# Where the empty rows are written: one scatter per group of the ranking, or all of them in the first softmax

## What is computed

```python
K, Q, V = typed_linear(x, Wk, ...), typed_linear(x, Wq, ...), typed_linear(x, Wv, ...)
att,   v   = edge_msgs(K[row], Q[col], V[row], e1, e2)   # row = src, col = dst
att_i, v_i = edge_msgs(K[col], Q[row], V[col], e2, e1)   # the inverse edges
att   = seg_softmax(att, col, n)      # over the edges with the same dst
att_i = seg_softmax(att_i, row, n)    # over the edges with the same src
agg = segment_sum(v * att, by=col) + segment_sum(v_i * att_i, by=row)
...
return _layernorm(x + layer(agg, x))
```

## Time and profile before

| | us |
|---|---|
| median of 3 runs | 9991.26 |
| lowest, highest | 9989.2, 9998.15 |
| profiled execution | 9994.34 |
| its span, first to last instruction | 9992.6 |

### The profile page before, as it was taken

The page is one execution under the profiler, slowest core; times in us unless marked ns, Lnnn a source line. Parts: engine busy times, 40 slices in busy tenths (PEclk is TensorE's granted clock), DMA queues, the critical chain, the costliest instruction groups (busy, mean ns, idle before and its releaser), DMA issues. The chain is left out here.

```text
span 9992.6 us, 137436 instructions
## 1 busy us (share of the span) xinstructions
PE 6360.8 (64%) x34016; PEld 4321.0 (43%) x34017; DVE 6541.9 (65%) x13906; ACT 4360.4 (44%) x13243; POOL 5689.7 (57%) x5436
## 2 busy tenths in 40 slices
PE   3778666666665577677767677621677643899543
PEld 1257444444443344444444444410555432677322
DVE  1068999999997566666666666652555537888523
ACT  0100433344433455555555555521555543888411
POOL 4230777777777577777777777756888800000022
PEclk6655555555555788888888888865988877999755
DMA  3110000000000788888888888876999994787510
GB/s 100 43 51 2 8 9 9 9 9 9 9 9 9 244 262 261 263 259 261 260 261 258 261 260 258 255 197 210 334 332 332 322 131 135 254 259 258 197 43 23
DMA packets 1355142, 1664.99 MB, mean 167 GB/s; under 512 B 418366, under 2 KB 1154898, under 8 KB 1354722
## 3 DMA queue, kind: packets, MB, share of 16 engines
q1 hardware_dynamic: 854746, 958.02, 29.4%
q0 software_dynamic: 260288, 671.32, 21.8%
q10 hardware_dynamic: 239946, 34.12, 3.3%
HBM read 1059.06 MB, written 641.81 MB: 170 GB/s over the span
## 5 line engine op out<-in xcount | busy, mean ns | idle before, releaser
L1118 PE MATMUL exch_pG<-exch_tab,exch_ohT 128*128 x3328 | 1528.4, 616 | 953.7 <-ACT exch_kc L1040 949.3
L1541 PE MATMUL sum_pS<-sum_row,sum_oh 128*128 128x260 f32 x6656 | 1670.8, 408 | 698.3 <-issue 292.3
L985 POOL DMA_INDIRECT exch_row<-table,exch_of x1664 | 1676.2, 1007 | 551.0 <-issue 507.9
L830 POOL DMA_INDIRECT recs<-place_rec,place_addr x1568 | 1598.5, 1019 | 509.2 <-issue 485.6
L1541 PEld LDWEIGHTS sum_pS<-sum_row,sum_oh 128*128 128x128 f32 x6656 | 1309.7, 202 | 1059.0 <-issue 856.0
L1118 PEld LDWEIGHTS exch_pG<-exch_tab,exch_ohT 128*128 128x128 f32 x3328 | 768.1, 242 | 1696.8 <-issue 1502.2
L1580 DVE TENSOR_TENSOR sum_row<-sum_row,agg_al 128x1792 f32<-128x1792 f32 x416 | 841.4, 2023 | 510.1 <-DMA sum_row<-spill 496.9
L1199 POOL DMA_INDIRECT bys<-sum_pb x768 | 949.5, 1236 | 273.6 <-issue 225.3
L1199 POOL DMA_INDIRECT bys<-exch_pb x832 | 841.2, 1011 | 312.2 <-issue 248.2
L1563 ACT ACTIVATE sum_off<-kept_ramp,sum_neg 128x128 f32<-128x128 f32 x3328 | 1017.6, 388 | 0.0
L784 DVE SCALAR_TENSOR_TENSOR place_junk<-place_pB,place_own_g,sort_tri 128x128 bf16<-128x128 f32 x3136 | 879.8, 347 | 15.3 <-issue 15.2
(11 more groups left out here) (297 smaller groups left out, 12097.1 us busy)
## 6 DMA issues: line engine op xcount, KB each, us to landing
spill<-exch_row SPq DMA_DIRECT2D x208, 1024.0 KB, 5.1
sum_row<-spill SPq DMA_DIRECT2D x208, 1024.0 KB, 7.8
sum_row<-bys SPq DMA_DIRECT2D x208, 1024.0 KB, 4.9
mid<-exch_pb SPq DMA_DIRECT2D x208, 528.0 KB
sum_pb<-mid SPq DMA_DIRECT2D x192, 528.0 KB, 4.6
exch_row<-table,exch_of POOLq DMA_INDIRECT x1664
recs<-place_rec,place_addr POOLq DMA_INDIRECT x1568
bys<-exch_pb POOLq DMA_INDIRECT x832
```

Source lines behind the costliest of these rows:

```text
L830: nc.gpsimd.indirect_dma_start(recs, bass.IndirectOffsetOnAxis(addr[:, par, 0, t:t + 1], 0), rec[:, par, t, :], None, bounds_check=last_sl ...
L985: nc.gpsimd.indirect_dma_start(row[q][:, t, TD:TD + S.TW], None, table, bass.IndirectOffsetOnAxis(of[q][:, t:t + 1], 0), bounds_check=last ...
L1118: nc.tensor.matmul(pG[t % 3][:, 0:VK], ohT[ring(j, 2)][:, t, :], flat[:, bass.ds(tiles[t] * GW, VK)], start=True, stop=True).then_inc(s_ga ...
L1541: last = nc.tensor.matmul(pS[h * HG + t // 2][:, 0:AW], oh[h][:, t, :], row[j][:, t, :], start=(t % 2 == 0), stop=(t % 2 == 1))
```

## The change

The counting stage works out the same list of empty slots, now in a tile `pad_at`, and SyncE writes it to a new DRAM tensor, `free`. The placing stage no longer scatters empty rows: no four ahead of group 0, no 17th scatter in a group, no copy of 128 slot numbers on ScalarE, no tile `none`, and the waits count 16 scatters. In the first softmax SyncE loads the list ahead of the keys, VectorE fills a tile `none` with the empty row ahead of its other work, and GpSimd scatters it 102 times, ahead of the 64 scatters that it has there. At the end of that stage GpSimd waits for these too.

```diff
@@ -493,7 +493,9 @@
                 sp.dma_start(r[:, n * w:(n + 1) * w, :], padrec[:]).then_inc(s_pad, 16)
             sp.wait_ge(s_hc, 3)
             sp.dma_start(otile1, otile[1][:]).then_inc(s_pad, 16)
-            sp.wait_ge(s_pad, 144)
+            sp.wait_ge(s_free, 1)
+            sp.dma_start(free, pad_at[:]).then_inc(s_pad, 16)
+            sp.wait_ge(s_pad, 160)
 
         @block.scalar
         def _(act):
...
@@ -580,7 +582,7 @@
                     link(nc.vector.tensor_scalar(pad_h[:], pad_h[:], 7, None, ALU.logical_shift_right))
                     link(nc.vector.scalar_tensor_tensor(out=pad_l[:], in0=pad_l[:], scalar=float(NT), in1=pad_h[:],
                                                         op0=ALU.mult, op1=ALU.add))
-                    link(nc.vector.tensor_tensor(k.padslot[:], pad_l[:], pad_off[:], ALU.add))
+                    nc.vector.tensor_tensor(pad_at[:], pad_l[:], pad_off[:], ALU.add).then_inc(s_free, 1)
 
                 dve.wait_ge(s_ot, d + 1)
                 for n in range(4):
...
@@ -646,9 +647,6 @@
             s.sem(n) for n in ("stage", "oh", "rowp", "rows", "tps", "tlo", "l", "selr", "addr", "link", "turn", "rec", "whole")]
         s_b, s_eq, s_cnt, s_cur, s_low = [[s.sem(f"{n}{d}") for d in range(2)] for n in ("b", "eq", "cnt", "cur", "low")]
         s_scat = [s.sem(f"scat{p}") for p in range(2)]
-        none = s.sb("none", [P, S.RC])
-        pad_at = s.sb("pad_at", [P, 2, 1], I32)
-        s_none, s_pads = s.sem("none"), s.sem("pads")
         block = ctx.enter_context(nc.Block())
 
         @block.scalar
...
@@ -677,8 +675,7 @@
                 if more:
                     act.wait_ge(s_addr, g + 1)
                     stage(g + 1, 1 - par)
-                act.wait_ge(s_scat[par], i * (16 * (SG + 1)))
-                nc.scalar.activation(pad_at[:, par, :], k.padslot[:, bass.ds(g, 1)], ACT.Copy)
+                act.wait_ge(s_scat[par], i * (16 * SG))
                 nc.scalar.activation(rec[:, par, :, 0:3], ln[:, bass.ds(g * SG, SG), :], ACT.Copy)
                 nc.scalar.activation(rec[:, par, :, S.OWN], own[:, 0, bass.ds(g * SG, SG)], ACT.Copy)
                 nc.scalar.activation(rec[:, par, :, S.LO], piece[:, 0, 0, bass.ds(g * SG, SG)], ACT.Copy)
...
@@ -751,9 +748,6 @@
 
         @block.vector
         def _(dve):
-            nc.vector.memset(none[:], 0.0).then_inc(s_none, 1)
-            dve.wait_ge(s_none, 1)
-            nc.vector.memset(none[:, S.SC + S.H:S.SC + S.H + 1], -1.0).then_inc(s_none, 1)
             nc.vector.memset(rec[:], 1.0)
             nc.vector.memset(piece_g[:], 0.0).then_inc(s_addr, 1)
             nc.vector.memset(slot[:], 0.0).then_inc(s_selr, 1)
...
@@ -803,7 +797,7 @@
                 nc.vector.tensor_scalar(slot_l[:], slot_i[:], P - 1, None, ALU.bitwise_and)
                 link(nc.vector.tensor_scalar(slot_i[:], slot_i[:], 7, None, ALU.logical_shift_right))
                 link(nc.vector.scalar_tensor_tensor(out=slot[:], in0=slot_l[:], scalar=float(NT), in1=slot_i[:], op0=ALU.mult, op1=ALU.add))
-                dve.wait_ge(s_scat[par], i * (16 * (SG + 1)))
+                dve.wait_ge(s_scat[par], i * (16 * SG))
                 link(nc.vector.tensor_tensor(addr[:, par], slot[:], bc(inval[:, bass.ds(g * SG, SG)], 1, 2), ALU.add))
                 nc.vector.tensor_copy(rec[:, par, :, S.SLOT].bitcast(I32), addr[:, par, 1, :]).then_inc(s_addr, 1)
                 assert n_link[0] == PER, n_link
...
@@ -812,15 +806,6 @@
         @block.gpsimd
         def _(pool):
             last_slot = nc.gpsimd.to_reg(P * NT - 1)
-
-            def pad(at, sem):
-                nc.gpsimd.indirect_dma_start(bys, bass.IndirectOffsetOnAxis(at, 0), none[:], None,
-                                             bounds_check=last_slot, oob_is_err=False).then_inc(sem, 16)
-
-            pool.wait_ge(s_none, 2)
-            pool.sem_inc(s_turn, 1)
-            for n in range(NG, S.NPC):
-                pad(k.padslot[:, n:n + 1], s_pads)
 
             def body(g, par, i, more):
                 pool.wait_ge(s_rec, g + 1)
@@ -830,11 +815,9 @@
                     nc.gpsimd.indirect_dma_start(recs, bass.IndirectOffsetOnAxis(addr[:, par, 0, t:t + 1], 0),
                                                  rec[:, par, t, :], None, bounds_check=last_slot,
                                                  oob_is_err=False).then_inc(s_scat[par], 16)
-                pad(pad_at[:, par, :], s_scat[par])
             in_turns(pool, NG, body)
-            pool.wait_ge(s_pads, 16 * (S.NPC - NG))
             for par in range(2):
-                pool.wait_ge(s_scat[par], (NG // 2) * 16 * (SG + 1))
+                pool.wait_ge(s_scat[par], (NG // 2) * 16 * SG)
 
 
 def angle_table(nc, k, S, s, w_time, b_time, blk):
...
@@ -1225,7 +1208,9 @@
         s_in, s_a, s_dve, s_sub, s_exp, s_c, s_t, s_e, s_f, s_k, s_x = [
             s.sem(n) for n in ("in", "a", "dve", "sub", "exp", "c", "t", "e", "f", "k", "x")]
         if bys is not None:
-            s_turn = s.sem("turn")
+            s_turn, s_none, s_free, s_pads = [s.sem(n) for n in ("turn", "none", "free", "pads")]
+            none = s.sb("none", [P, S.RC])
+            pad_at = s.sb("pad_at", [P, S.NPC], I32)
             pb = [s.sb(f"pb{n}", [P, S.LATER, S.RC]) for n in range(8)]
             s_pb, s_sc = [[s.sem(f"{n}{j}") for j in range(8)] for n in ("pb", "sc")]
         block = ctx.enter_context(nc.Block())
@@ -1235,6 +1220,8 @@
         @block.sync
         def _(sp):
             kv = keys.rearrange("t e -> (t e)")
+            if bys is not None:
+                sp.dma_start(pad_at[:], free).then_inc(s_free, 16)
             sp.wait_ge(s_k, 1)
             sp.dma_start(key[:, 1:C + 1], kv[0:SPn * C].rearrange("(p c) -> p c", p=SPn)).then_inc(s_in, 16)
             if SPn > 1:
...
@@ -1272,6 +1259,12 @@
         def _(pool):
             if bys is not None:
                 last_slot = nc.gpsimd.to_reg(P * S.NT - 1)
+                pool.wait_ge(s_none, 2)
+                pool.wait_ge(s_free, 16)
+                pool.sem_inc(s_turn, 1)
+                for n in range(S.NPC):
+                    nc.gpsimd.indirect_dma_start(bys, bass.IndirectOffsetOnAxis(pad_at[:, n:n + 1], 0), none[:], None,
+                                                 bounds_check=last_slot, oob_is_err=False).then_inc(s_pads, 16)
                 for n in range(S.AHEAD):
                     pool.wait_ge(s_pb[n % 8], 16 * (n // 8 + 1))
                     pool.sem_inc(s_turn, 1)
@@ -1279,6 +1272,7 @@
                         forward(nc, S, pb[n % 8], t, bys, last_slot).then_inc(s_sc[n % 8], 16)
                 for n in range(8):
                     pool.wait_ge(s_sc[n], 16 * S.LATER * (S.AHEAD // 8))
+                pool.wait_ge(s_pads, 16 * S.NPC)
 
         @block.scalar
         def _(act):
...
@@ -1294,6 +1288,10 @@
         @block.vector
         def _(dve):
             link, _ = chain(dve, s_dve)
+            if bys is not None:
+                nc.vector.memset(none[:], 0.0).then_inc(s_none, 1)
+                dve.wait_ge(s_none, 1)
+                nc.vector.memset(none[:, S.SC + S.H:S.SC + S.H + 1], -1.0).then_inc(s_none, 1)
             link(nc.vector.memset(zero[:], 0.0))
             link(nc.vector.memset(key[:, 0:1], -2.0))
             nc.vector.memset(key[:, C + 1:C + 2], -2.0).then_inc(s_k, 1)
...
@@ -1836,6 +1834,7 @@
     mid = nc.dram_tensor("mid", [P, S.NT, S.RC], F32, kind="Internal").ap()
     bys = nc.dram_tensor("bys", [P * S.NT, S.RC], F32, kind="Internal").ap()
     runs = nc.dram_tensor("runs", [P, S.NT, S.H + 1], F32, kind="Internal").ap()
+    free = nc.dram_tensor("free", [P, S.NPC], I32, kind="Internal").ap()
     otile1 = nc.dram_tensor("otile1", [1, S.NT], I32, kind="Internal").ap()
     keys = [nc.dram_tensor(f"keys{d}", [S.NT2, P], F32, kind="Internal").ap() for d in range(2)]
     att = [nc.dram_tensor(f"att{d}", [S.NT2, S.H, P], F32, kind="Internal").ap() for d in range(2)]
```

More of the change, by code:

```diff
@@ L419, in one_hots, with sort_edges @@
     return last
-def sort_edges(nc, k, S, src, dst, edge_attr, recs, otile1, bys):
+def sort_edges(nc, k, S, src, dst, edge_attr, recs, otile1, free):
     CT, SG, NO = S.CT, S.SG, S.NO
@@ L471, in count_owners @@
         pad_h = s.sb("pad_h", [P, NPC], I32)
+        pad_at = s.sb("pad_at", [P, NPC], I32)
         pH = [s.pb(f"pH{d}") for d in range(2)]
         pO = [s.pb(f"pO{n}") for n in range(4)]
-        s_in, s_ea, s_dve, s_c, s_oh, s_h, s_hc, s_o, s_oc, s_ot, s_rec, s_pad, s_prep = [
-            s.sem(n) for n in ("in", "ea", "dve", "c", "oh", "h", "hc", "o", "oc", "ot", "rec", "pad", "prep")]
+        s_in, s_ea, s_dve, s_c, s_oh, s_h, s_hc, s_o, s_oc, s_ot, s_rec, s_pad, s_prep, s_free = [
+            s.sem(n) for n in ("in", "ea", "dve", "c", "oh", "h", "hc", "o", "oc", "ot", "rec", "pad", "prep", "free")]
         block = ctx.enter_context(nc.Block())
@@ L612, in _, with place_edges @@
                 last.then_inc(s_ot, 1)
```

(9 more changed lines are left out.)

7 lines of the change are left out of this document (3 added, 4 removed).

## The result

The changed kernel takes 10043.1 us (median of 6 runs, 10035.8 to 10048.5), the kernel before 9990.2 beside it (6 runs): ratio 1.0054, 95% interval 1.0041 to 1.0067. It is slower by some 53 us; 37 were forecast. The profiled run takes 10048.3 us, with a span of 10046.6 where the earlier trace rows has 9992.6. In a later batch it was 1.0060 (1.0041 to 1.0079).

A forecast was written before the change was run, and what follows sets the result against it. Placing was taken as bound by a two-group loop through the scatters' landing, near GpSimd's own rate. Terms −89.7 − 1.3 − 0.4 + 0.7 + 128.0 gave +37.3 us, 10028.6 us on the median; range 9983 to 10060.

The forecast's parts named there:

- part 4: First softmax: 102 uncovered scatters at 1.276 us add 130.2, an earlier start takes off 2.2; sum +128.0 us.
- part 5: First softmax: exponentials wait behind loads needing scatter 134, but weights are out near 6890, hidden before GpSimd ends at 6911.
- part 1: Placing: without 98 pad scatters the two-group loop falls from 22.555 to 21.63 us a group, gaining 89.7 us, plus 1.3.
- The landing of a record scatter: Placing: time from a record scatter's end until ScalarE may start; 1.28 us forecast, bounds 1.13 and 1.58.
- The hold: Placing: GpSimd scatters held while VectorE builds one-hots; 1.08 us a group forecast, bounds 0.33 and 1.36.
- The rule of the Trainium skill: Placing: VectorE wouldn't stop descriptor writing, so hold 0, step 21.09 us and whole change about −15 us.
- Placing, mean step: Placing: group-to-group step falls from 22.555 to 21.63 us over 97 steps, gaining 89.7 us.
- Start: Before the first record scatter: dropped `none` fills −0.4 us, the list's store in counting +0.7.
- A: Rival: placing gains nearly all, holds 0.33, quick landing, step 21.2 us; whole −4 us, 9987; chance 27 in 100.
- B: Rival: VectorE's own 20.88 us sets placing's step; stage gains 162, whole −35 us, 9956; chance 7 in 100.
- C: Rival: landing 1.58, hold 1.36, placing step 21.92 us; whole +65, 10057; chance 64 in 100 together with the forecast.
- D: Rival: the removed scatter wasn't on placing's path, which gains nothing; whole +128, 10119; chance 2 in 100.

The follow-up runs named there:

- the rows in both places: Kernel before with its placing scatters kept, plus all 102 empty-row scatters in the first softmax: 10123.3 us, ratio 1.0125.
- four buffers: Changed kernel with four buffers of `rec` and `addr` in placing instead of two, loop body of four groups: 10051.1 us, ratio 1.0048 to the kernel before.
- the spread one: Changed kernel with 41 of 102 empty-row scatters moved from the first softmax to two other stages; other chips: 12167.9 and 12172.3 us, ratios 0.9937 and 0.9943.
- 17 scatters: Changed kernel plus a seventeenth 32-byte-row scatter per group in placing, to an unread spare tensor; another chip: 12365.7 us, kernel before 12258.5.

## Why the prediction was right, and where it was off

Sign and range held; the size was 37 for 53. That it comes so near is in part luck: by the profiles the terms of the change and its surroundings add up to 63 us, and an output stage that no term spoke of takes 11 off again.

- **Softmax, part 4**: +128.0 forecast, +128.9 by the profiles, +128.3 with the rows in both places. That the 102 scatters have no cover and that VectorE's scans take in as many scatters as before (102 of them take 1417 ns on average, the 64 behind them 976) was read rightly: the time over 0.973 us a scatter is 45.3 us in all, before (64 scatters) as after (102). The first scatter comes 2.84 us after the stage's first DMA, for 4.02 before; that is −1.2 where −2.2 was forecast. The exponentials come 222 us after the stage's start (215 forecast), behind ScalarE's last loads, and GpSimd is still the last: part 5 holds.
- **Placing, part 1, steady step**: 21.63 forecast, 21.57 measured. The landing of a record scatter was set at 1.28 from row sizes; it is 1.29 (1474.97, the end of the last scatter of group 20, to 1476.26 on ScalarE); that it is the row size that makes it shorter than the pad's 1.58 was not tested by itself. The hold was set at 1.08 a group; the mean is 16 x (1.031 − 0.975) = 0.9. With four buffers the step falls to VectorE's 20.88, so it is the landing that closes the loop. The rule of the Trainium skill that was weighed (SBUF — State Buffer, Who interferes with whom), by which no hold should be and the whole come to −15, is against these rows: the mean record scatter went up from 1019 to 1031 ns, not down.
- **Placing, mean step**: this is the term that was mis-sized. 97 x 0.925 = 89.7 was to be gained, 76 to 78 came. Steady groups gave 97 x 0.985 = 95.5, but 13 gaps of 1.92 us more than the usual 0.30 took 13 x 1.4 = 18 back: seven groups with a gap take 152.4 us in place of 7 x 21.57 = 151.0, and the mean step is 21.75. The placing of before has no such gap, and no bound of mine held one; its trace has a single one of 2.00 us, between two scatters of the projection (487.48), that I passed over.
- **Placing's end**: 6.0 us that weren't in the sum. SyncE starts 11.5 us after the last scatter instead of 5.5, in the changed kernel's two profiles and in both of the spread one; 6.3 with four buffers and two groups behind the loop, 5.1 with 17 scatters. The landing takes 1.2 of the 11.5. The difference is GpSimd's `DRAIN`: 9.21 us in place of 2.84, and 3.98 with four buffers. So the place of these 6 us is found, and what the `DRAIN` does in them is open.
- **Start**: +1.8 for +0.3; 1.5 of it lie ahead of the changed code (SyncE's store of `otile1` is issued at 987.1 for 985.6), and kernels with the same code there issue it anywhere from 984.4 to 989.4. So these 1.5 us aren't the change's.
- **The rest**: exchange and sums +4.7, within what two profiles of one kernel differ by. Whether the output stage's −10.8 is the change's is open: its code is the same, but both profiles of before have 555 us and both of the changed kernel 544 (below). Without it the change costs 63 us here by the profiles.
- **Rivals**: A (holds stay small, −4) fell, since the mean hold is 0.9 and GpSimd waits for VectorE in 82 groups. B's 20.88 was seen, but only with four buffers. C's landing of 1.58 was not. D (placing gains nothing) fell here.

## What to carry to other kernels

A step moved off a loop gives back only the share with which it stands in the loop's longest chain, here about 0.8 us of a 1.28 us scatter, and pays its full price where nothing covers it; write down both chains before counting instructions. If work is to go out of a loop, spread it over stages by measured idle time and check which engine's late end it moves, since here 41 moved scatters gave 59 us in one stage and took 17 in two others. Before unrolling a loop for more buffers, price a turn of the longer body (3 us on VectorE here) against what the buffers save.

## What the hardware showed that was not expected

- **GpSimd stops for 2.23 us between two scatters, after the 113th and every 112th behind it**, in both profiles of the changed kernel and both of the spread one, so always behind the first scatter of a group, every seventh one; with four buffers it is 1.48 us and every 80th, whether the loop's body has 4 or 16 groups; with 17 scatters a group, wide or narrow, never in placing. It isn't the loop's turn, which comes every 32nd, 64th or 256th. It isn't a load of instructions either: from 1030 to 3080 us, with 13 such stops, the changed kernel's DMA list has the queue of the scatters and no other:

```profile
q0 software_dynamic: 48192, 6.26, 2.8%
```

  It goes together with the long `DRAIN` at the stage's end, which is 9.21 us in the kernels with the stop of 2.23, 3.98 with 1.48 and 2.84 without a stop. The cause is open.
- **A turn of a long loop body costs 2.9 us on VectorE** with a body of 4 groups, 2.9 to 3.3 in the step, and none with a body of 2. With a body of 16, on other chips, it is up to 3.9 in the step, but not at each turn.
- **The output stage takes 544, 555 or 566 us with the same code.** The stretches of a fifth of it, with granted clock behind the busy times (PE, PEld, DVE, ACT, POOL), for its first fifth in the kernel before, the changed one and the one with four buffers:

```profile
9437.00:9550.00 113.00, 53.34 (x135) 32.41 (x136) 24.49 (x98) 19.87 (x62) 33.39 (x31) 0.53 0.29 94
```
```profile
9502.00:9611.00 109.00, 42.75 (x136) 26.73 (x136) 30.49 (x120) 22.12 (x71) 33.46 (x31) 0.61 0.30 98
```
```profile
9484.00:9597.00 113.00, 53.63 (x126) 32.23 (x127) 24.44 (x98) 19.87 (x62) 33.35 (x31) 0.50 0.29 94
```

  Some 135 matmuls take 42.8 us at a granted clock of 0.61 and 53.3 at 0.53. In the second sum TensorE is busy in 744 of 800 us (8600 to 9400, the changed kernel) at a granted clock of 1.0 (2.4 GHz). Then it has nothing to do, and some 83 us ahead of this stage the clock falls to 0.5 (1.2 GHz), in each of these profiles. What differs is how much of 1.0 comes back within the stage: 65 us in all in the changed kernel, 48 in the one before, 34 with four buffers. That repeats: 555.3 and 555.2 us in the two profiles of before, 544.5 and 544.4 in those of the changed kernel. On the other chips one kernel can differ by 7 us (548.2, 554.8 and 555.3 in the widest spread). So it isn't shown whether a change ahead of this stage moves it or chance does. 22 us lie between the ends, as much as all that a measurement can tell here, so this stage is best looked at by itself when two profiles are compared.
- **Three other chips are slower by 23% with the same code**: the kernel before takes 12244 to 12274 us there. The kernels that were profiled lose it in placing (31.1 us a group), with TensorE's matmuls 0.5 to 1.2 us apart while GpSimd issues scatters, and in the exchange with the building of the runs (4651 to 4701 us for 3424). Both sums with the second softmax, in which GpSimd issues 768 scatters, take 2648 to 2672 us there and 2647 to 2657 here, so scatters alone don't do it. One scatter more a group costs 1.65 us a group there, though GpSimd idles 10.
